# A two-layer adaptive-norm transformer kernel: the normed input of the attention laid out batch by batch, value products in lots of sixteen, and the ends of the expert chunks made by GpSimd

## What is computed

```python
h = _layernorm(x) * (1 + ca) + sa
# attention of layer 0, after a second layernorm with ln_gamma, ln_beta
q = (xn @ Wq.T + bq); k = (xn @ Wk.T + bk); v = (xn @ Wv.T + bv)
content_score = einsum('bthd,bshd->bhts', q + u_bias, k)
pos_score = _rel_shift(einsum('bthd,phd->bhtp', q + v_bias, p))
attn = softmax((content_score + pos_score) / sqrt(dh))
x = x + ga * (einsum('bhts,bshd->bthd', attn, v) @ Wout.T + bout)
# mixture of 8 experts, hidden size 256, the best 2 of 8 weighted
h = _layernorm(x) * (1 + cb) + sb
g, u = einsum('nd,ehd->neh', h, w_gate), einsum('nd,ehd->neh', h, w_up)
y = einsum('neh,edh->ned', silu(g) * u, w_down)
x = x + gb * einsum('ned,ne->nd', y, combine)
```

## Time and profile before

| | |
|---|---|
| median of 3 timed runs | 1176.24 us (1173.62 to 1180.53) |
| profiled execution | 1182.93 us, span 1181.1 us |
| busy in the span | PE 914.0, DVE 774.5, ACT 470.2, POOL 328.1 us |
| mean granted TensorE clock | 0.869 |
| stages | projections to 90, first operands to 136, heads to 508, experts 587 to 862 us |

### The profile page before, as it was taken

The page is one execution under the profiler, slowest core; times in us unless marked ns, Lnnn a source line. Parts: engine busy times, 40 slices in busy tenths (PEclk is TensorE's granted clock), DMA queues, the critical chain, the costliest instruction groups (busy, mean ns, idle before and its releaser), DMA issues.

```text
span 1181.1 us, 22636 instructions
## 1 busy us (share of the span) xinstructions
PE 914.0 (77%) x8587; PEld 673.7 (57%) x8587; DVE 774.5 (66%) x1594; ACT 470.2 (40%) x764; POOL 328.1 (28%) x364
## 2 busy tenths in 40 slices
PE   2594779999999999954699999999927870267774
PEld 1224668888888888733365555565513770245553
DVE  6553535455555545237788888888886758966673
ACT  4750123333333333336465555565553124122221
POOL 5624003342343334227200000000054035422332
PEclk7697789999999999976599999999968995578776
DMA  5056212332233233420000000000000000000000
GB/s 128 0 154 188 44 35 57 70 82 68 60 90 71 62 81 74 132 51 0 1 1 1 0 0 0 0 0 0 0 16 0 1 1 19 0 0 18 18 18 18
DMA packets 69588, 46.10 MB, mean 39 GB/s; under 512 B 35056, under 2 KB 60856, under 8 KB 68792
## 3 DMA queue, kind: packets, MB, share of 16 engines
q1 hardware_dynamic: 52776, 24.75, 9.1%
q0 software_dynamic: 8032, 19.11, 6.2%
q10 hardware_dynamic: 8704, 1.19, 0.6%
HBM read 30.05 MB, written 12.06 MB: 36 GB/s over the span
## 4 chain that ended last, share of the span: by engine, by line
PE 54%; DVE 20%; ACT 7%; POOL 5%; issue 5%; SPq 4%; DMA 3%; ACTq 1%; DVEq 0%; POOLq 0%
PE PS L916 9%; PE PS L991 6%; PE PS L993 5%; PE PS L992 5%; PE PS L936 5%; PE PS L896 4%; PE PS L920 4%; PE PS L897 4%; PE PS L854 3%; PE PS L1111 2%; PE PS L1127 2%; SPq L312 2%; DVE STAT L1156 2%; DVE HB L1395 2%; POOL HN L479 2%
## 5 line engine op out<-in xcount | busy, mean ns | idle before, releaser
L1266 DVE TENSOR_REDUCE MX<-PS 128x2 f32<-128x512 f32 x256 | 171.3, 686 | 169.9 <-PE PS L897 168.2
L693 ACT ACTIVATE REG<-PS 128x1024 f32<-128x1024 f32 x128 | 131.4, 1027 | 242.0 <-PE PS L920 239.2
L916 PE MATMUL PS<-XX,TB 96*128 96x64 f16 x2048 | 159.6, 246 | 3.9 <-DMA XX<-NEG 3.9
L896 PE MATMUL PS<-TM,YY 128*128 128x256 f16 x512 | 129.2, 284 | 26.7 <-DMA YY<-REG 11.2
L916 PEld LDWEIGHTS PS<-XX,TB 96*128 96x128 f16 x2048 | 130.7, 120 | 32.3 <-issue 19.4
L897 PE MATMUL PS<-KM,YY 128*128 128x256 f16 x512 | 126.3, 279 | 0.0
L736 ACT ACTIVATE SG<-PS 128x512 f32<-128x512 f32 x128 | 76.3, 597 | 106.5 <-PE PS L993 106.2
L991 PE MATMUL PS<-XH,XX 128*128 (+1 forms) x256 | 99.4, 388 | 24.3 <-DVE HB L1395 24.3
L1395 DVE SCALAR_TENSOR_TENSOR HB<-PS,SG 128x512 f32<-128x512 f32 x128 | 87.4, 688 | 35.7 <-ACT SG L736 33.5
L920 PE MATMUL PS<-XX,KC 97*128 97x128 f16 x1024 | 107.1, 228 | 0.0
L992 PE MATMUL PS<-XH,XX 128*128 (+1 forms) x256 | 99.1, 387 | 0.0
(11 more groups left out here) (220 smaller groups left out, 1746.3 us busy)
## 6 DMA issues: line engine op xcount, KB each, us to landing
REG<-inverse_sums POOLq DMA_DIRECT2D x60, 128.0 KB, 2.9
YY<-queries_content ACTq DMA_DIRECT2D x224, 4.0 KB
KC<-keys_strips SPq DMA_DIRECT2D x16, 192.0 KB
keys_strips<-REG POOLq DMA_DIRECT2D x12, 224.0 KB, 8.1
R<-in_L_attn_x SPq DMA_DIRECT2D x32, 64.0 KB, 2.7
out<-R SPq DMA_DIRECT2D x64, 32.0 KB, 1.6
queries_position<-REG POOLq DMA_DIRECT2D x2, 960.0 KB, 8.4
queries_content<-REG POOLq DMA_DIRECT2D x2, 960.0 KB, 15.0
```

The source lines that it names most:

```text
L693: A(P[jt][:, 1024 * up:1024 * up + 1024].rearrange("p (k x) -> p k x", k=2), ST[u % 2], ACT.Exp).then_inc(exp_done, 1)
L896: mm(o, yp[:, a], TM[p][:, 31 - a:31 - a + T], start=True, stop=False)
L916: mm(o_pos[:, a], TB[p][0:96, y0:y0 + 128], xp[0:96, 8 * bank + a], start=(a == 0), stop=False, skip_group_check=True)
L1266: nc.vector.tensor_reduce(MX[h % 2][:, 2 * kk:2 * kk + 2], banks[4 + kk % 2].rearrange("p (a j) -> p a j", a=2), AX_X, ALU.max)\
```

## The change

Three edits. (1) `R1` is laid out batch by batch when it is written (view `BY_BATCH`); K, content queries and value projections read it contiguously, position queries in runs of 32 tokens. Their results now come batch by batch too, so that the stores to `NAT` turn the order (`natural`), while the one to `NQB` doesn't. (2) The two halves of `context_part` follow each other, behind steps 4 and 12. (3) GpSimd takes the gate product, the copy of the next weights and the addition to `R2` at the end of each expert chunk.

```diff
+        BY_BATCH = R1[:, :].rearrange("p (b i) -> p b i", b=B)
+        def natural(c, part):
+            kind, chunk, bank = projection(c)
+            to = NAT[2 * kind + part][:, 512 * chunk:512 * chunk + 512]
+            if kind == 1:
+                return to.rearrange("p (i b) -> p i b", b=B), bank.rearrange("p (b i) -> p i b", b=B)
+            return to, bank
...
-            sp.wait_ge(cmbt, 24)
+            sp.wait_ge(moe_added, 8)
...
-            gp.wait_ge(cmbt, 24)
+            def add_experts(tc):
+                gp.wait_ge(acc_done, 8 * tc + 10)
+                gp.tensor_tensor(ACC2[:, :, :], ACC[:, :, :], MOD[0][:, 5, :].unsqueeze(1).to_broadcast([128, 4, D]),
+                                 ALU.mult).then_inc(acc_free, 1)
+            def combine_weights(tc):
+                gp.tensor_copy(CMBT[:, :, :], CMB[:, bass.ds(4 * tc, 4), :]).then_inc(cmbt, 1)
+            def expert_residual(tc):
+                gp.wait_ge(acc_free, tc + 1)
+                x4 = R2[:, bass.ds(4 * tc, 4), :]
+                gp.tensor_tensor(x4, x4, ACC2[:, :, :], ALU.add).then_inc(moe_added, 1)
+                gp.wait_ge(moe_added, tc + 1)
+            gp.wait_ge(weights_ready, 1)
+            combine_weights(0)
+            with gp.Fori(0, 7) as tc:
+                add_experts(tc)
+                combine_weights(tc + 1)
+                expert_residual(tc)
+            add_experts(7)
+            expert_residual(7)
...
-                    A(R1[:, 512 * c:512 * c + 512], banks[4 + c % 2][:, :], ACT.Identity,
+                    A(BY_BATCH[:, :, 32 * c:32 * c + 32], banks[4 + c % 2].rearrange("p (i b) -> p b i", b=B), ACT.Identity,
...
-                A(NAT[2 * kind][:, 512 * chunk:512 * chunk + 512], bank, ACT.Identity,
-                  bias=VEC3[:, kind:kind + 1]).then_inc(high_done, 1)
+                A(*natural(c, 0), ACT.Identity, bias=VEC3[:, kind:kind + 1]).then_inc(high_done, 1)
...
-                   (R1_bi[:, 8 * (chunk % 2) + chunk // 2:8 * (chunk % 2) + chunk // 2 + 5:4, :],
-                    R1[:, 512 * chunk:512 * chunk + 512], R1_bi[:, 2 * chunk:2 * chunk + 2, :])[kind],
+                   (BY_BATCH[:, 8 * (chunk % 2) + chunk // 2:8 * (chunk % 2) + chunk // 2 + 5:4, :],
+                    BY_BATCH[:, :, 32 * chunk:32 * chunk + 32], BY_BATCH[:, 2 * chunk:2 * chunk + 2, :])[kind],
...
-                              R1_bi[:, b, 128 * jt:128 * jt + 128], WVT[:, :], start=True, stop=True)
+                              BY_BATCH[:, b, 128 * jt:128 * jt + 128], WVT[:, :], start=True, stop=True)
...
-                    if h and k in (3, 6):
-                        context_part(h - 1, 1, int(k == 6))
-                    if k in (11, 14):
-                        context_part(h, 0, int(k == 14))
+                    if h and k == 4:
+                        context_part(h - 1, 1, 0)
+                        context_part(h - 1, 1, 1)
+                    if k == 12:
+                        context_part(h, 0, 0)
+                        context_part(h, 0, 1)
...
-                STT(NAT[2 * kind + 1][:, cols], bank, VEC3[:, kind:kind + 1], NAT[2 * kind][:, cols],
+                STT(low, product, VEC3[:, kind:kind + 1], natural(c, 0)[0],
...
-            def weigh(tc, e):
+            def weigh(tc, e, first=False):
                 ve.wait_ge(y_mm, 8 * tc + e + 3)
                 if e:
                     ve.wait_ge(acc_done, 8 * tc + e + 2)
+                else:
+                    ve.wait_ge(cmbt, tc + 1)
+                    if not first:
+                        ve.wait_ge(acc_free, tc)
...
-                    elif e == 1:
-                        if not first:
-                            finish(tc - 1)
-                            ve.wait_ge(cmbt, 3 * tc)
-                        nc.vector.tensor_copy(CMBT[:, :, :], CMB[:, bass.ds(4 * tc, 4), :]).then_inc(cmbt, 1)
-                        ve.wait_ge(cmbt, 3 * tc + 1)
+                    elif e == 1 and not first:
+                        weigh(tc - 1, E - 1)
...
-            finish(7)
-            ve.wait_ge(cmbt, 24)
+            weigh(7, E - 1)
+            ve.wait_ge(moe_added, 8)
```

More of the change, by code:

```diff
@@ L201, in adaln_program @@
         khi_first, k_first, khi_out, k_out, qvb_out, qv_out, qu_out, pos_out, ones_set, w_low, hb_done, hi_done, x_high, f_round, l_tr, l_ev, root_done, centred, scale_done, mod_ready, bias_done, o_mul, l_mul = (sem(s) for s in ("khi_first", "k_first", "khi_out", "k_out", "qvb_out", "qv_out", "qu_out", "pos_out", "ones_set", "w_low", "hb_done", "hi_done", "x_high", "f_round", "l_tr", "l_ev", "root_done", "centred", "scale_done", "mod_ready", "bias_done", "o_mul", "l_mul"))
-        cmbt, loop_dve = sem("cmbt"), sem("loop_dve")
+        weights_ready, cmbt, acc_free, moe_added, loop_dve = (sem(s) for s in (
+            "weights_ready", "cmbt", "acc_free", "moe_added", "loop_dve"))
         loop_per = [0]
@@ L629, in projected @@
                     A(NQB[:, :].rearrange("p (b i) -> p b i", b=B)[:, :, 32 * chunk:32 * chunk + 32],
-                      bank.rearrange("p (i b) -> p b i", b=B), ACT.Identity, bias=VEC3[:, 1:2])
-                A(NAT[2 * kind][:, 512 * chunk:512 * chunk + 512], bank, ACT.Identity,
-                  bias=VEC3[:, kind:kind + 1]).then_inc(high_done, 1)
+                      bank.rearrange("p (b i) -> p b i", b=B), ACT.Identity, bias=VEC3[:, 1:2])
+                A(*natural(c, 0), ACT.Identity, bias=VEC3[:, kind:kind + 1]).then_inc(high_done, 1)
             def centre(k, src, dst, done, before=0):
@@ L1247, in _ @@
                 kind, chunk, bank = projection(c)
-                cols = slice(512 * chunk, 512 * chunk + 512)
+                low, product = natural(c, 1)
                 ve.wait_ge(high_done, c + 1)
-                STT(NAT[2 * kind + 1][:, cols], bank, VEC3[:, kind:kind + 1], NAT[2 * kind][:, cols],
+                STT(low, product, VEC3[:, kind:kind + 1], natural(c, 0)[0],
                     ALU.add, ALU.subtract).then_inc(stage, 1)
@@ L1375, in _ @@
             step(TT(CMB[:, :, :], LG[1][:, :, :], LG[3][:, :, :], ALU.add))
-            step(TS(CMB[:, :, :], CMB[:, :, :], 1.0 / WS, None, ALU.mult))
-            def weigh(tc, e):
+            TS(CMB[:, :, :], CMB[:, :, :], 1.0 / WS, None, ALU.mult).then_inc(weights_ready, 1)
+            def weigh(tc, e, first=False):
                 ve.wait_ge(y_mm, 8 * tc + e + 3)
@@ L1399, in low_hidden @@
                 TT(HH[k % 4][:, 1, :], HB[k % 2][:, :], HH[k % 4][:, 0, :], ALU.subtract).then_inc(h_done, 1)
-            def finish(tc):
-                weigh(tc, E - 1)
-                ve.wait_ge(acc_done, 8 * tc + 10)
-                TT(ACC2[:, :, :], ACC[:, :, :], MOD[0][:, 5, :].unsqueeze(1).to_broadcast([128, 4, D]), ALU.mult).then_inc(cmbt, 1)
-                ve.wait_ge(cmbt, 3 * tc + 2)
-                x4 = R2[:, bass.ds(4 * tc, 4), :]
-                TT(x4, x4, ACC2[:, :, :], ALU.add).then_inc(cmbt, 1)
             def chunk(tc, first):
@@ L1417, in chunk @@
                         weigh(tc - 1, E - 2)
-                    elif e == 1:
-                        if not first:
-                            finish(tc - 1)
-                            ve.wait_ge(cmbt, 3 * tc)
-                        nc.vector.tensor_copy(CMBT[:, :, :], CMB[:, bass.ds(4 * tc, 4), :]).then_inc(cmbt, 1)
-                        ve.wait_ge(cmbt, 3 * tc + 1)
+                    elif e == 1 and not first:
+                        weigh(tc - 1, E - 1)
                     elif e > 1:
-                        weigh(tc, e - 2)
+                        weigh(tc, e - 2, first)
                 low_hidden(tc, 15)
```

## The result

Four timed executions of the change gave a median of 1158.88 us (1158.31 to 1160.12), four of the kernel before 1175.05 us (1173.62 to 1180.53): ratio 0.9855, 95% interval 0.9821 to 0.9890, 16 us. Forecast were 1161 us, 1149 to 1171.

The account below looks back on a forecast made before the run. TensorE was taken to bound attention and expert loop, the chain from projections into SyncE's small DMAs the part ahead. -5.5 - 4.6 - 5.4 = -15.5 us took 1176.24 to 1160.7, said as 1161, range 1149 to 1171.

Parts of the forecast that it names:

- Front: Projections and DMAs ahead of the attention: contiguous reads of `R1` and joined DMA bursts, -5.5 us (bounds -1 and -9).
- The sub-step on the stores: Position-query stores to `NAT`: a step of 16 halves costs 0.44 us more on ScalarE, 0.55 on VectorE, per store.
- Lots: Attention: value products in lots of sixteen instead of eight, -4.6 us (bounds -7 and -2).
- The switch of 0.24 us: Attention: a lot of sixteen value products costs TensorE 1.96 us instead of 2.20, 0.24 less per merge.
- head 14's row: Row of negated maxima, issued later and behind the expert weights: 1.5 us lost (bounds 0.9 and 3.4).
- Ends of chunks: Expert chunk ends: GpSimd takes over VectorE's multiply, copy and add, -5.4 us (bounds -13.2 and +1).
- so 0.96 us per chunk remain: Expert loop: gain per chunk after VectorE's waiting for GpSimd, 0.96 us, seven times: -6.7 us.
- the plain count: Expert loop: removed VectorE work without waiting for GpSimd, -2.07 us per chunk, -14.5 in seven.
- the one in which GpSimd costs nothing: Rival, expert loop: VectorE loses nothing to GpSimd, the loop gives 13.2, total -23 us, 1153; chance 0.18.
- the one in which it takes all back: Rival, expert loop: `HB` and `weigh` wait too or GpSimd's additions take 1.75 us; -9 to -10, 1167; chance 0.12.
- the one in which the front gives nothing: Rival, front: joined bursts slow SyncE's first DMAs, or stores cost more than doubled; -10 us, 1166; chance 0.13.
- the slower one: Rival, attention: the row of negated maxima is late in every head, 1.5 us in each of 14; 1182; chance 0.04.

Follow-up runs that it names:

- Experiment 3: The change with the position queries' stores to `NAT` turned, a step of 16 halves on the store and the bank read in order: 1170.14 us, ratio 0.9946.
- experiment 5: The change with SyncE issuing the expert weights only when the last row of negated maxima has landed: 1153.35 us, ratio 0.9808.
- Experiment 7: The change with GpSimd multiplying and adding only one column of 128 at the chunk ends, for its times alone: 1154.01 us, ratio 0.9817.

## Why the prediction was right, and where its steps were not

**Front: 5.5 us forecast, 5.2 measured (layout alone), 6 to 7 in the traces.** Right in its main steps: matmuls at 0.43 to 0.45 us, bursts joined, SyncE's list moved. The sub-step on the stores failed: results "are written to `NAT` with a step of 16 halves", for which I charged 0.44 and 0.55 us. I had not followed the order in which the two views iterate. The store is in order, the bank's read has the step, and such a read was in the kernel before: its store to `NQB` read the bank with a step of 16 floats in 0.68 us, as long as the one to `NAT` behind it. ScalarE's timeline before:

```profile
40.78 0.68 ACT L629 ACTIVATE NQB<-PS,VEC 128x512 f16<-128x512 f32 x1
41.35 0.68 ACT L631 ACTIVATE REG<-PS,VEC 128x512 f16<-128x512 f32 x1
```

So ScalarE's list didn't grow by 1.8 us, SyncE's copies moved by 5 us and not 1.6, and the last low part ended at 77.3 us, not near 80. That this moved the second head by only 1 to 1.5 us more than forecast is the DMA bound that the prediction put behind it: SyncE's eight loads took 2.5 us more than before in the joined burst. Experiment 3 shows what a true step on the store costs: 10.5 us in all, which would have left the change near the "within 0.5%" case. That 5.5 came so near 5.2 is then luck in part: a cost that wasn't there and a SyncE list that came earlier than forecast stood against loads slower than forecast.

**Lots: 4.6 forecast, 3.9 measured.** The switch of 0.24 us is confirmed: heads 0.47 us closer, and the waits that I had called just covered cost nothing. For head 14's row I had 1.5 us; the two last heads take 34.6 to 35.4 us in the seven traces that have the lots and the old place of the loads, and 35.0, 32.3 and 31.4 in the three without lots. That is 2.2 us between the means, but the layout alone has 35.0 with halves at steps 11 and 14, so how much of it the lots cause stays open. TensorE's wait for the row speaks for a part: 4.3 to 4.6 us in the seven, 2.3, 3.6 and 1.8 in the three. Shown by experiment 5 is that the change loses 5 to 6 us there to the loads ahead of the row, more than the 2.2 us between the means; the prediction saw the place and priced only what the lots add. The 0.86 us at head 0 can't be told from the spread of the DMAs: heads 0 and 1 take 58.4, 58.7 and 59.2 us in the traces without lots, and 59.7 with the lots alone.

**Ends of chunks: 5.4 forecast, 9.3 measured alone (6.9 to 11.6), 8.2 in the traces.** The mechanism is right in each step; the step "so 0.96 us per chunk remain" is mis-sized: a chunk gained 1.34 us. I had put GpSimd's copy behind the low half and 0.1 us between operations; the copy was under way already and ended 0.07 us behind the half, so the addition ended 3.21 us after the weighted sum, not 3.49, and `HB` of step 6 and TensorE behind it were 0.4 us earlier in all. Seven chunks give 9.4 us, and 1.2 are added behind the last `HB` (8.4 instead of 7.2 us to the statistics), as forecast (1.3). Experiment 7 puts the rest of the contention at 0.75 us a chunk: with it gone the chunk is 2.09 us shorter than before, the 2.07 of the plain count. The Trainium skill's rule ("SBUF — State Buffer", Who interferes with whom), that a VectorE instruction with two SBUF inputs and a GpSimd one that reads SBUF exclude each other, is what the trace shows: 1.38 us instead of 0.68.

**Sum.** 5.5 + 4.6 + 5.4 = 15.5 forecast, 16 measured; by the single edits the terms were 0.3 less, 0.7 less and 3.9 more, 18.4, of which the whole kept 16 to 17. That the sum came within 1 us is luck in part: the ends gave 3.9 more than forecast, and together the edits gave 1 to 2 us less than one by one, which their intervals don't separate from nothing. Of the rivals, the one in which GpSimd costs nothing (-13.2 in the loop) was refuted by the waits of 0.74 us, the one in which it takes all back by the chunks' distance, the one in which the front gives nothing by the layout alone (5.2 us, 3.5 to 6.8), the slower one by rows that land in 2.1 us in the median and make TensorE wait only in head 15.

## What to carry to other kernels

Read a pair of views as the order in which one instruction walks both sides, and put the step on the side where it is free: here a PSUM read by ScalarE or VectorE; on an SBUF store of halves it made the instruction over three times as long. Work moved to GpSimd beside a busy VectorE costs by how many of VectorE's two-input SBUF instructions meet it; short pieces let them pass. A small DMA on the critical path wants to be issued, and landed, ahead of the big loads that nobody waits for yet: one wait gave 6 us.

## What the runs showed of the hardware that I had not expected

- A store of halves with a step of 16 takes 2.10 us (ScalarE) and 2.12 us (VectorE) for 128x512, against 0.57 and 0.66 in order; a store of floats with the same count of steps 0.88 against 0.60.
- A PSUM read with a step of 32 floats costs neither engine anything (0.57 and 0.67 us).
- GpSimd waits for VectorE as VectorE does for it: its copy of 128x32 took 0.68 us beside a low half and 0.21 with none; its second product 1.60 instead of 1.27.
- With the same instructions in front, the second head's first maxima stood between 133.2 and 136.9 us in the three traces of the old layout and between 126.0 and 130.1 in the nine of the new one (turned stores aside), and a chain of four small DMAs took 10.1 to 14.2 us.
